# Quantised weights, head norms, masks and memsets moved between the engines of a twelve-part decoder

## The reference

```python
# l1x: 16 query heads of 128, 4 key groups; 128 context keys and 128 own keys a sequence
q = rms_norm((x @ wq).reshape(B, L, 16, 128), q_norm_w)   # over the 128 of each head
k = rms_norm((x @ wk).reshape(B, L, 4, 128), k_norm_w)
k_ctx = rms_norm((ctx @ wk_ctx).reshape(B, T, 4, 128), k_norm_w)
q = q * cos + rotate_half(q) * sin                          # k likewise
scores = einsum(q, concat([k_ctx, k])) / sqrt(128) + mask   # causal on the own keys
out = (softmax(scores) @ concat([v_ctx, v])) @ wo

# l2f
def act_quant(x):
    scale = 127.0 / clip(max(abs(x), axis=-1), EPS)
    return round(clip(x * scale, -128.0, 127.0)) / scale
def weight_quant(w):
    scale = 1.0 / clip(mean(abs(w)), EPS)
    return round(clip(w * scale, -1.0, 1.0)) / scale
def bitlinear(x, w):
    return einsum('bsi,oi->bso', act_quant(rmsnorm(x)), weight_quant(w))
bitlinear(silu(bitlinear(x, w_gate)) * bitlinear(x, w_up), w_down)   # 256 -> 1024 -> 256
```

## Time and profile before

| | |
|---|---|
| time, median of 3 runs | 1761.83 us (1760.81 to 1770.02) |
| the profiled execution's own time | 1759.31 us |
| span of the profile | 1757.2 us |
| busy: PE, DVE, ACT, POOL | 1532.9 (87%), 1062.9 (60%), 755.8 (43%), 142.6 (8%) |
| share of the chain that ended last: PE, DVE, ACT, issue, POOL | 63%, 24%, 6%, 4%, 2% |
| transfers | 48.14 MB, 27 GB/s mean |

### The profile page before, as it was taken

How to read it: one execution, slowest core, us unless ns; L and a number is a source line. 1 busy time by engine, 2 the same in 40 slices (tenths; PEclk the granted TensorE clock), 3 DMA queues, 4 the chain that set the end, 5 groups by cost and what they waited for, 6 DMA issues and landing times.

```text
span 1757.2 us, 26171 instructions
## 1 busy us (share of the span) xinstructions
PE 1532.9 (87%) x10016; PEld 967.9 (55%) x10016; DVE 1062.9 (60%) x1990; ACT 755.8 (43%) x1774; POOL 142.6 (8%) x160
## 2 busy tenths in 40 slices
PE   5859999998999889999999978799964599999788
PEld 2535555564566456666667845646641445556546
DVE  5774222225576688777885867536768875585631
ACT  2352111112766466565653544356655244262220
POOL 1130000000000000000000010000000204314200
PEclk9988999999899999999999979779986689999979
DMA  7020110003000200000001000010010100000000
GB/s 223 7 90 1 59 54 27 1 1 144 1 2 2 108 7 7 7 7 7 7 1 66 1 20 1 1 72 2 2 63 1 48 1 1 3 0 2 26 1 24
DMA packets 21647, 48.14 MB, mean 27 GB/s; under 512 B 1426, under 2 KB 16787, under 8 KB 20372
## 3 DMA queue, kind: packets, MB, share of 16 engines
q1 hardware_dynamic: 21524, 46.47, 7.6%
HBM read 41.22 MB, written 5.24 MB: 26 GB/s over the span
## 4 chain that ended last, share of the span: by engine, by line
PE 63%; DVE 24%; ACT 6%; issue 4%; POOL 2%; DMA 0%; SPq 0%; DVEq 0%; ACTq 0%; POOLq 0%
PE PS L584 49%; PE PS L771 5%; DVE work L2000 4%; PE PS L641 4%; PE PS L1051 2%; PE PS L596 1%; DVE work L1890 1%; DVE work L1892 1%; DVE WA L1888 1%; DVE WA L1887 1%; DVE WA L1907 1%; DVE small L1588 1%; DVE small L1929 1%; POOL XN L563 1%; DVE XN L1601 1%
## 5 line engine op out<-in xcount | busy, mean ns | idle before, releaser
L584 PE MATMUL PS<-XT,WB 128*128 128x512 f32 x656 | 301.6, 609 | 0.0
L584 PE MATMUL PS<-work 128*128 128x256 f32 (+7 forms) x688 | 170.9, 389 | 37.6 <-DVEq L1903 19.8
L584 PEld LDWEIGHTS PS<-XT,WB 128*128 128x128 f32 x656 | 125.5, 196 | 141.4 <-issue 138.9
L1296 ACT ACTIVATE work<-PS,small 128x128 f32<-128x128 f32 x512 | 141.0, 415 | 80.8 <-DVE small L1823 80.8
L584 PEld LDWEIGHTS PS<-work 128*128 128x128 f32 (+4 forms) x688 | 96.3, 189 | 98.5 <-issue 38.7
L1797 DVE TENSOR_TENSOR work<-PS,work 128x512 f32<-128x512 f32 x48 | 33.1, 692 | 171.2 <-PE PS L584 171.2
L584 PE MATMUL PS<-XT,WA 128*128 128x512 f32 (+1 forms) x248 | 115.2, 619 | 1.9 <-DVEq L2003 1.9
L1258 ACT ACTIVATE work<-PS 128x512 f32<-128x512 f32 x48 | 28.7, 597 | 194.1 <-PE PS L584 194.1
L1823 DVE TENSOR_REDUCE small<-PS 128x4 f32<-128x512 f32 x128 | 82.3, 685 | 43.9 <-PE PS L584 43.9
L510 POOL TENSOR_SCALAR small<-small 128x4 f32<-128x4 f32 x24 | 6.5, 273 | 1137.6 <-DVE small L1591 1137.6
L584 PE MATMUL PS<-WA,XT 128*128 128x256 f32 (+2 forms) x416 | 89.0, 376 | 4.7 <-DVE XT L1843 3.0
(11 more groups left out here) (353 smaller groups left out, 2730.3 us busy)
## 6 DMA issues: line engine op xcount, KB each, us to landing
WB<-in_l0f SPq DMA_DIRECT2D x8, 768.0 KB, 7.8
WB<-in_l1x SPq DMA_DIRECT2D x1, 6144.0 KB, 16.9
WB<-in_l0f SPq DMA_DIRECT2D x32, 96.0 KB, 6.9
WB<-in_l2f SPq DMA_DIRECT2D x1, 3072.0 KB, 10.1
WA<-in_l3a SPq DMA_DIRECT2D x1, 2624.0 KB, 8.9
WB<-in_l3f SPq DMA_DIRECT2D x1, 2064.0 KB, 7.8
WA<-in_l1f SPq DMA_DIRECT2D x1, 2056.0 KB, 10.0
C<-in_ctx SPq DMA_DIRECT2D x2, 1024.0 KB, 7.6
```

Source lines behind the costliest of these rows:

```text
L584: mm = lambda o, l, r, s, e: nc.tensor.matmul(o, l, r, start=s, stop=e)
L1296: f(wk(12288 + (u % 8) * G + h * P, P), bank(j)[:, h * P:(h + 1) * P], ACT.Exp, bias=sm(704 + (u % 8) * 4 + h, 1)).then_inc(*act_step(*([j ...
```

## The change

**l0x.** ScalarE scales the keys of block b - 1 behind the squares and values of block b, rather than those of block b behind its own.

**l1x.** One mask matmul a score bank, first in the bank, over the own-key halves of both heads. Heads 2 and 3 move to r = 1. All four norm sums are one job `rq` at r = 2: four matmuls, one for each head, in which 32 columns of ones are stationary and the 512 squares are moving, so that each head fills 32 partitions of the bank; a copy by ScalarE; a job `rt` at r = 3 that transposes it; a ScalarE copy of 16 columns; GpSimd adds a constant and takes the power -0.5. ScalarE's roots and DVE's reciprocal and scale are gone. DVE rotates all four heads in r = 0 and 1 and gives the new handoff `turned` there.

**l2x and l2f.** ScalarE's three sums of absolute weights stand amid l2x's heads, PE adds them over partitions (`ws`) at step 20 of its plan, DVE makes scales, and GpSimd makes the quantised weights, nine passes of 128 x 2048, into a place of their own (`wq`). PE waits for `weights_ready` before the gates. In l2f DVE works by groups of four blocks; GpSimd makes the root of the mean square from the variance that is there already, so ScalarE's squares and root go; the clamp of the activations to -128 and 127 goes (|x * scale| is at most 127 by its scale). The second scales are made by group as well, the first within the loop over blocks, and GpSimd takes their root.

**l3a and l2a.** GpSimd's memsets start later: for l3a behind the last layernorm transposes, for l2a behind the last `z` job.

```diff
-            l += [[("k", w), ("q", w, 0), ("q", w, 1)], [("k2", w), ("rq", w, 0)],
-                  [("q", w, 2), ("q", w, 3)], [("rq", w, 1)]][r]
+            l += [[("k", w), ("q", w, 0), ("q", w, 1)], [("k2", w), ("q", w, 2), ("q", w, 3)], [("rq", w)], [("rt", w)]][r]
@@ GpSimd, l1x
+                nc.gpsimd.tensor_scalar(sm(768 + lo, 16), sm(768 + lo, 16), P * 1e-6, None, ALU.add).then_inc(pool_own, 1)
...
+                nc.gpsimd.tensor_tensor(sm(640 + lo, 16), sm(768 + lo, 16), head_power, ALU.pow).then_inc(head_roots.sem, head_roots.give())
@@ GpSimd, amid l2x
+            for i, n in enumerate(("gate", "up", "down")):
+                w = W(WB, W_L2F, n)
+                for step in range(3):
...
+                        ins = nc.gpsimd.tensor_scalar(w, w, sm(139 + i, 1), MAGIC, ALU.mult, ALU.add)
...
+                        ins = nc.gpsimd.tensor_scalar(w, w, MAGIC - 1.0, MAGIC + 1.0, ALU.max, ALU.min)
...
+                        ins = nc.gpsimd.tensor_scalar(wq[:, i * 2048:(i + 1) * 2048], w, MAGIC, None, ALU.subtract)
@@ GpSimd, l3a
-            pool.wait_ge(*freed(job_of[("l2f",) + plan["l2f"][-1]]))
-            for i in range(4):
-                nc.gpsimd.memset(l3a_x(i), 0.0).then_inc(windows_zero, 1)
+            roots()
             pool.wait_ge(halves_ready, 5)
             pool.wait_ge(steps_ready, 1)
             pool.wait_ge(*full(job_of["l3a", "ln", 1, 1]))
+            for i in range(4):
+                nc.gpsimd.memset(l3a_x(i), 0.0).then_inc(windows_zero, 1)
@@ PE, l1x
-                        pe.wait_ge(dve_to_pe.sem, dve_to_pe.next())
+                        pe.wait_ge(turned.sem, turned.next())
...
+                        mm(r3(o, D)[:, :, P:D], identb[:, :], r3(causalb[:, 0:2 * P], P), True, True)
...
-                            ins = mm(o[:, i * D + P:(i + 1) * D], identb[:, :], causalb[:, 0:P], False, True)
...
+                        for h in range(4):
+                            ins = mm(o[32 * h:32 * h + 32, :], cst("ones")[:, 0:32], l1x_sq(1 + h), True, True)
@@ ACT, l0x
                     evict_to(J("l0x", "vc", b))
+                if 1 <= b <= NB:
+                    x = b - 1
+                    j = J("l0x", "kc", x)
                     act.wait_ge(key_roots.sem, key_roots.next())
@@ ACT, amid l2x
+                    if layer == "l2x" and key[0] == "s" and key[1] in (20, 26, 32):
...
+                        f(WB[:, 9216:9216 + 2048], W(WB, W_L2F, ("gate", "up", "down")[i]), ACT.Abs, accum_out=sm(128 + i, 1)).then_inc(weight_sums, 1)
@@ DVE, l1x, prepare(w, r)
-                if r % 2 == 1:
+                for hh in ((0, 1), (2, 3), (), ())[r]:
                     dve.wait_ge(act_to_dve.sem, act_to_dve.next())
-                    rq = sm(640 + (w % 4) * 16 + (r // 2) * 8, 8)
-                    v.reciprocal(rq, rq).then_inc(*dve_step())
...
+                    rotate(r3(l1x_q(w, hh), P), qcos, qsin)
+                if r == 1:
+                    dve.sem_inc(turned.sem, turned.give())
@@ DVE, l2f
             for b in range(NB):
                 hb = wk(b * 1024, 1024)
                 v.tensor_scalar(hb, hb, sm(168 + b, 1), MAGIC, ALU.mult, ALU.add).then_inc(*dve_step())
                 dve.wait_ge(*dve_last())
-                v.tensor_scalar(hb, hb, MAGIC - 128.0, MAGIC + 127.0, ALU.max, ALU.min).then_inc(*dve_step())
-                dve.wait_ge(*dve_last())
                 v.tensor_scalar(wkb(14336, 8192)[:, b * 1024:(b + 1) * 1024], hb, MAGIC, None, ALU.subtract).then_inc(*dve_step(dve_to_pe))
```

251 lines of the change are left out of this document (140 added, 111 removed).

## The result

The changed kernel takes 1736.01 us (median of 4 runs, 1735.14 to 1736.73), the kernel before 1761.32 beside it: a ratio of 0.9846, 95% interval 0.9824 to 0.9868. That is 25 us less, where 12 were forecast. The range of 1729 to 1767 holds it, but the gain is twice the forecast's. The profiled span fell from 1757.2 to 1733.4.

What follows compares the result with a forecast made beforehand. TensorE was busy for most of the span, with limits differing by sublayer; l1x's round was bound 11.74 us by it, 30.34 by DVE. −7.9 + 25 − 20.6 − 6.6 = −10.1, −12 with (b) and l2a: 1761.8 to 1750, range 1729 to 1767.

Steps and rivals of the forecast that it cites:

- (c): In l1x, both rotations ahead of the third normalisation stall TensorE 7.3 us a round; plain rounds become 46.4 us.
- l1x: The whole stage was to take 25 us longer, or 8 longer without clock drops.
- (b): In l1x, one mask of 256 columns instead of two of 128: zero, with up to 1 us kept in the range.
- (a): In l1x, norm sums by four 32-row matmuls and four transposes: TensorE gains 2.2 us a round, hidden in the new stall.
- l3a, with l2a: Later GpSimd memsets no longer slow DVE's normalisations: −6.6 us in l3a; l2a's smaller gain left in the range.
- l0x and l2f: l0x: output transposes begin earlier, −7.9 us; l2f: shorter DVE chains before, in and behind the loop, −20.6 in the sum.
- The cover: GpSimd's nine weight passes, from about 1255, take 16 to 39 us and end by 1294, ahead of l2f's gates at 1320.5.
- GpSimd's passes holding up DVE in the heads: Slower rival in l2x: DVE waits for the weight passes, 16 to 39 us more, 1766 to 1789 us; 13%.
- No drop of the clock: Rival: l1x's stalls cost no clock, so l1x +8 and total −29, 1733 us; 12%.
- The reordering pays: Rival: P isn't late, TensorE sets l1x's rounds at about 37 us, l1x loses 35 to 40, 1690 us; 5%.

Runs made afterwards that it cites:

- e3: The changed kernel with only heads 2 and 3 rotated by DVE one step later, where the kernel before rotated them; 1710.21 us.
- e15: The changed kernel with the kernel before's two mask matmuls of 128 columns behind the scores instead of one of 256 ahead; 1739.47 us.
- e1: The changed kernel with DVE in l1x scaling P and copying its transposes before the window's rotations in each step; 1744.38 us.
- e5: The changed kernel with DVE's l1x rotations spread over the round's four steps and the key's preparation put behind the scaling of P; 1689.53 us.
- e10: e5 with ScalarE instead of DVE copying the first half of transposed P out of PSUM; 1685.43 us.
- e14: The changed kernel with sixteen tiny DVE memsets, about 3.6 us, ahead of l0f and nothing else; 1740.12 us.
- e11: The kernel before with only the l0x part of the change; 1753.48 us, 0.9946 of the kernel before.
- e12: The changed kernel with l0x, l1x and the memsets of l2a and l3a as in the kernel before; 1737.30 us, ratio 0.9851.
- e8: The changed kernel with other operations, operands and types the same, in GpSimd's second and third weight pass; 1738.48 us, one run.

## Why the prediction was right in its parts and wrong in its sum

**(c), the order in l1x: right.** Forecast: a stall of 7.3 for the scaling of P, near 11 in the first round, six rounds of 283.3 us. Measured: 7.68 to 8.34 and 11.02; the six rounds from 637.17 to 918.35 take 281.2. One of the seven stalls came out at 4.9, for the copy of transposed P, and a wait of 5.4 for rotated heads stayed before the first round, where none was forecast. The granted clock in the 4 to 5 us behind each stall was 0.50 in four of them and 0.62 to 0.66 in the other three; the three jobs took 5.7 to 7.2 us (722.36 to 729.40 is 7.04), 45.8 behind all seven, where 4.16 + 2.4 each make 45.9. That the order is the cause is shown by e3.

**(b), the mask: the first term that failed.** It stood at 0 to 1 us, because the columns are the same in number. The measured worth is 5.0 [e15], and l1x beat its term by 4.8. The mask's columns do cost the same: the starts of the records give them 0.22 to 0.23 us a step in either kernel. The scores between take 1.73 instead of 1.89. That is the side that the prediction had kept at up to 1 us, "fewer weight switches"; e15 changes the number of masks and their place together, so which of the two makes it is not shown. That 5.0 and 4.8 agree so well is in part luck: 281.2 and six times 0.61 are 1.5 over the forecast for the six rounds, and behind the last stall 1.8 went that nobody had forecast. In the kernel before, the step behind the wait of 2.93 at 904.70 took 8.21 us, at a granted clock of 0.60 up to 909, and the next like it 6.44; in e15, whose code there is the same, that stretch is 1.8 shorter.

**(a)**: four 32-row matmuls and four transposes took 0.99 and 0.60 us, where 1.13 and 0.45 were forecast, and stand ahead of the stall, which hides their gain.

**l3a, with l2a: the second term that failed.** −6.6 was only the time by which DVE's two normalisations were longer beside the memsets (the lock, for short). Behind the stall of TensorE for them, 6.58 us [the 1399.19 row of before], the granted clock is 0.50, and 32 projections take 7.06 us instead of 3.76. For l1x I had charged a stall with the clock it costs; for l3a and l2a I priced the same kind of stall without it. Over all kernels l3a took 258.5 us in the mean of four with the early memsets (257.5 to 259.9) and 247.0 in the mean of fourteen without (243.9 to 250.5). So the edit is worth 11.5, and its fellow in l2a 3.3 to 3.5. From the first transposes to the projections it takes 10.7 in the mean of the four and 4.1 in that of the fourteen: 6.6, the very term of the forecast. Of the other 4.9 the projections hold 2.2. The last 2.7 come behind them, and no experiment took them apart. Without the stall the clock may still be low there: it was in e1, e5, e10 and e14, where the projections took 7.06 as well.

**l0x and l2f: right**, shown by e11 and e12. In l2f the gates begin 12.67 us after the normalisation instead of 26.18 (−13.5, forecast −13.3), the passes over hidden features take 13.13 instead of 17.97 (−4.8, forecast −4.8), the loop between them 26.2 from gates to passes instead of 29.6 (−3.4, forecast −2.1). Together with l2x that is −21.4 where −20.6 was forecast.

**The cover: held, on a bound that didn't, and so partly by luck.** Nine passes took 44.0 us, where 16 to 39 was the range: 1.98, 7.08 and 5.38, not 2 to 3. They began at 1265.5, not 1255, and ended at 1309.5, not by 1294: 8.6 us before l2f's normalisation and 21 before the gates, which wait for them. The stages are indifferent to 26 us of them [e8].

**The rivals.** GpSimd's passes holding up DVE in the heads: no. From l2x's first transposes to l2f's normalisation 160.6 us passed with the passes and 160.4 without. No drop of the clock: no, it fell behind every stall. The reordering pays: not in the order that the change chose; in e5's it does, with l1x at 340.1, 27 below before. The forecast's reason, that a stall comes, was right. The rival's number of 37 us for a round that TensorE sets was reached by none; e10's 38.4 still has a wait of 1.4 in it.

**The sum.** It was −10.1 and, with 1 each for (b) and l2a, −12. Add −3.8 for l1x, the mask's gain beyond that 1 as far as l1x shows it, −4.9 for l3a by the means, −2.5 for l2a: −23.2. The profiles' difference is −23.8, the medians' −25.3. So half of the gain was missing from the forecast, and nearly all of that in terms that had been put at nothing or near it: the mask, and what TensorE loses in l2a and l3a once it has waited for DVE beside GpSimd's memsets. What then remains, l2f −0.8, l1a −1.0, l1f +2.5 and the last us of l3a, is of the size that e14 moves by a bare delay.

## What to carry to other kernels

A step moved ahead on an engine that is nearly full is charged with everything that comes behind it: not only who waits for its result, but who waits for the buffers that the work behind it frees. Where a stall of TensorE goes or comes, price its clock with it, each time and not only where the sum needs it: in l2a the lock was a third of the cost and the slower projections behind it two thirds. Single profiles of two kernels can't tell an effect of a few us on a stage whose code is the same; a bare delay, as a control run, shows how far such a stage moves by itself.
